# Half tiles of V as the unit of flow in a graph layer kernel

## What is computed

```python
h = relu(layernorm(x, axis=-1))
q = einsum('c,bcn->bn', wq, h)
k = einsum('c,bcn->bn', wk, h)
scores = q[:, None, :] + k[:, :, None]
scores = where(scores > 0, scores, 0.01 * scores)
att = softmax(scores, axis=-1)
agg = einsum('bcn,bmn->bcm', h, att)
out = x + relu(einsum('oc,bcm->bom', adj, agg) + bm[None, :, None])
```

## Time and profile before

| | us |
|---|---|
| median of 3 runs | 2064.33 |
| lowest, highest | 2063.56, 2064.44 |
| the profiled execution | 2065.63 |
| its span (first to last instruction) | 2063.6 |

### The profile page before, as it was taken

How to read it: one execution, slowest core, us unless ns; L and a number is a source line. 1 busy time by engine, 2 the same in 40 slices (tenths; PEclk the granted TensorE clock), 3 DMA queues, 4 the chain that set the end, 5 groups by cost and what they waited for, 6 DMA issues and landing times.

```text
span 2063.6 us, 37759 instructions
## 1 busy us (share of the span) xinstructions
PE 2035.2 (99%) x12467; PEld 1210.0 (59%) x12467; DVE 1721.7 (83%) x3631; ACT 1244.1 (60%) x2120; POOL 368.1 (18%) x272
## 2 busy tenths in 40 slices
PE   6999999999999999999999999999999999999999
PEld 5556556665566665566655666655666556666554
DVE  8988888888898888898888988888888889888863
ACT  5655756656656556566566565565665666655634
POOL 1012211112211122111121111221111211112212
PEclk9999999999999999999999999999999999999999
DMA  5244433334324444233443244442334432334322
GB/s 191 77 141 144 161 107 117 133 138 163 141 81 146 139 146 159 100 124 133 138 163 134 86 143 137 154 156 98 128 134 138 163 128 92 143 130 160 117 92 77
DMA packets 125119, 271.00 MB, mean 131 GB/s; under 512 B 21592, under 2 KB 22112, under 8 KB 120928
## 3 DMA queue, kind: packets, MB, share of 16 engines
q1 hardware_dynamic: 124480, 270.06, 37.8%
q10 hardware_dynamic: 544, 0.01, 0.0%
HBM read 202.38 MB, written 67.63 MB: 131 GB/s over the span
## 4 chain that ended last, share of the span: by engine, by line
PE 95%; DVE 3%; ACT 1%; DMA 1%; issue 0%; POOL 0%; SPq 0%; DVEq 0%; POOLq 0%
PE pair L450 21%; PE pair L451 21%; PE pair L452 21%; PE pair L421 11%; PE pair L426 10%; PE pair L424 10%; DVE den_out L794 1%; DMA ab_row<-ab_rows 0%; PE pair L344 0%; DVE p_ring L815 0%; ACT p_ring L546 0%; DMA xs<-in_x_dram 0%; PE small L399 0%; DVE v_lo L827 0%; DVE p_lo L822 0%
## 5 line engine op out<-in xcount | busy, mean ns | idle before, releaser
L450 PE MATMUL pair<-p_hi,v_hi 128*128 128x512 f16 x2048 | 776.4, 379 | 2.6 <-DVE p_lo L822 1.9
L452 PE MATMUL pair<-p_hi,v_lo 128*128 128x512 f16 x2048 | 776.2, 379 | 0.0
L451 PE MATMUL pair<-p_lo,v_hi 128*128 128x512 f16 x2048 | 776.2, 379 | 0.0
L997 POOL TENSOR_TENSOR res<-res,y 128x512 f32<-128x512 f32 x255 | 361.1, 1416 | 1674.5 <-ACT y L572 1674.5
L815 DVE SCALAR_TENSOR_TENSOR p_ring<-ab_row,cols,p_ring 128x512 f32<-128x512 f32 x512 | 376.6, 747 | 127.2 <-ACT p_ring L546 127.2
L794 DVE SCALAR_TENSOR_TENSOR den_out<-den_row,cols 128x512 f32<-128x512 f32 x512 | 440.7, 925 | 0.0
L546 ACT ACTIVATE p_ring<-ab_row,cols 128x512 f32<-128x512 f32 x512 | 353.2, 699 | 125.7 <-DMA ab_row<-ab_rows 125.7
L421 PE MATMUL pair<-wmT_hi,h_hi 128*128 128x258 f16 x2016 | 388.4, 273 | 3.1 <-ACT y L572 2.9
L424 PE MATMUL pair<-wmT_lo,h_hi 128*128 128x258 f16 x2016 | 386.6, 273 | 0.0
L426 PE MATMUL pair<-wmT_hi,h_lo 128*128 128x258 f16 x2016 | 386.5, 273 | 0.0
L822 DVE SCALAR_TENSOR_TENSOR p_lo<-p_ring,p_hi 128x512 f16<-128x512 f32 x512 | 349.7, 686 | 36.5 <-ACT p_hi L554 33.0
(11 more groups left out here) (97 smaller groups left out, 937.6 us busy)
## 6 DMA issues: line engine op xcount, KB each, us to landing
res<-in_x_dram SPq DMA_DIRECT2D x256, 256.0 KB, 3.3
out_dram<-res SPq DMA_DIRECT2D x256, 256.0 KB, 2.6
xs<-in_x_dram SPq DMA_DIRECT2D x124, 512.0 KB, 6.6
den_row<-den_rows SPq DMA_DIRECT2D x32, 1024.0 KB, 4.7
ab_row<-ab_rows SPq DMA_DIRECT2D x64, 512.0 KB, 4.8
res<-in_x_dram SPq DMA_DIRECT2D x4, 512.0 KB, 9.3
wm_nat<-in_adj_dram SPq DMA_DIRECT2D x4, 256.0 KB, 7.8
den_rows<-cols SPq DMA_DIRECT2D x32, 8.0 KB, 1.6
```

The lines of the kernel that those rows point to most:

```text
L450: pe.matmul(ps[:, :], v_hi[:, b[1], nt, chans], p_hi[:, hf, nt, :], start=(nt == 0), stop=False)
L451: pe.matmul(ps[:, :], v_hi[:, b[1], nt, chans], p_lo[:, hf, nt, :], start=False, stop=False)
L452: mm = pe.matmul(ps[:, :], v_lo[:, b[1], nt, chans], p_hi[:, hf, nt, :], start=False, stop=(nt == NT - 1))
L997: pool.tensor_tensor(res[:, k, :], res[:, k, :], y[:, k % 2, :], ALU.add).then_inc(s_add, 1)
```

## The change

Each bank of a V tile becomes a unit of its own. PE finishes the 12 matmuls of half 0 before those of half 1, and each half's last matmul increments s_v. ScalarE copies each half by itself (v_upper), VectorE splits each half by itself (v_lower), with one semaphore for each of the four banks, and PE waits for the bank alone before it writes to it again. The units 0 to 3 wait for their own bank (s_vlo[k]); unit 0's first two node tiles now wait for both halves of their V tiles. The start-up tiles (first_pass, second_pass, second_tiles, not shown) are signalled by half in the same way; their matmuls keep their order. In the first period alone, ScalarE does relus 5 and 6 before the two first leaks and relu 7 behind them, where they stood among the P tiles.

```diff
--- before.py
+++ after.py
@@ -181,7 +181,7 @@
         s_plo = sem("p_lo_ready")
         s_v = sem("v_psum_done")
         s_vhi = sem("v_hi_ready")
-        s_vlo = [sem(f"v_split_{i}") for i in range(2)]
+        s_vlo = [sem(f"v_split_{i}") for i in range(4)]
         s_acc = sem("unit_accumulated")
         s_y = [sem(f"relu_done_{i}") for i in range(2)]
         s_add = sem("unit_finished")
...
@@ -409,23 +409,19 @@
 
                 if nt == 0:
                     pe.wait_ge(s_hlo, cnt(b, CT, CT))
-                if nt < 2:
-                    for i in range(2):
-                        wait(pe, s_y[i], cnt(b, U // 2, nt + 3 - U))
-                else:
-                    pe.wait_ge(s_vlo[nt % 2], cnt(b, NT // 2, nt // 2))
                 ps, nodes = pair[nt % 2], slice(nt * P, (nt + 1) * P)
-                for ct in range(CT):
-                    hi, lo = h_hi[:, b[1], ct, nodes], h_lo[:, b[1], ct, nodes]
-                    for half, cols_of in enumerate((OH + QK, OH)):
-                        pe.matmul(ps[:, half, 0:cols_of], hi, wmT_hi[:, ct, half, 0:cols_of],
-                                  start=(ct == 0), stop=False)
-                    for half, cols_of in enumerate((OH + QK, OH)):
-                        pe.matmul(ps[:, half, 0:cols_of], hi, wmT_lo[:, ct, half, 0:cols_of], start=False, stop=False)
-                    for half, cols_of in enumerate((OH + QK, OH)):
-                        mm = pe.matmul(ps[:, half, 0:cols_of], lo, wmT_hi[:, ct, half, 0:cols_of],
-                                       start=False, stop=(ct == CT - 1))
-                mm.then_inc(s_v, 1)
+                for half, cols_of in enumerate((OH + QK, OH)):
+                    if nt < 2:
+                        wait(pe, s_y[half], cnt(b, U // 2, nt + 3 - U))
+                    else:
+                        pe.wait_ge(s_vlo[2 * (nt % 2) + half], cnt(b, NT // 2, nt // 2))
+                    for ct in range(CT):
+                        hi, lo = h_hi[:, b[1], ct, nodes], h_lo[:, b[1], ct, nodes]
+                        bank, w_hi, w_lo = ps[:, half, 0:cols_of], wmT_hi[:, ct, half, 0:cols_of], wmT_lo[:, ct, half, 0:cols_of]
+                        pe.matmul(bank, hi, w_hi, start=(ct == 0), stop=False)
+                        pe.matmul(bank, hi, w_lo, start=False, stop=False)
+                        mm = pe.matmul(bank, lo, w_hi, start=False, stop=(ct == CT - 1))
+                    mm.then_inc(s_v, 1)
 
             def unit(b, k, one, two):
 
@@ -434,7 +430,7 @@
                 if k >= MIX:
                     pe.wait_ge(s_y[k % 2], cnt(b, U // 2, (k - MIX) // 2 + 1))
                 elif one:
-                    pe.wait_ge(s_vlo[k // 2], cnt(nxt(b), NT // 2, NT // 2))
+                    pe.wait_ge(s_vlo[k], cnt(nxt(b), NT // 2, NT // 2))
                 else:
                     pe.wait_ge(s_y[k % 2], cnt(b, U // 2, (k + MIX) // 2 + 1 - U // 2))
                 ps, chans = mix[k % MIX], slice(ot * P, (ot + 1) * P)
@@ -444,7 +440,8 @@
                     if one and (k, nt) == ((1, 2) if at(b, first) else (0, 3)):
                         spread_qmax(nxt(b))
                     if k == 0 and nt < 2:
-                        pe.wait_ge(s_vlo[nt], cnt(b, NT // 2, NT // 2))
+                        for half in range(2):
+                            pe.wait_ge(s_vlo[2 * nt + half], cnt(b, NT // 2, NT // 2))
                     if ot == 0:
                         pe.wait_ge(s_plo, cnt(b, G, NT * hf + nt + 1))
                     pe.matmul(ps[:, :], v_hi[:, b[1], nt, chans], p_hi[:, hf, nt, :], start=(nt == 0), stop=False)
@@ -515,7 +512,7 @@
 
                 if ct == 0:
                     act.wait_ge(s_ln, cnt(b, LN_OPS, LN_OPS))
-                    wait(act, s_v, cnt(b, NT, -NT))
+                    wait(act, s_v, cnt(b, 2 * NT, -2 * NT))
                 src = x_second if at(b, second) else xs
                 act.activation(h_hi[:, b[1], ct, :], src[:, ct, :], ACT.Relu, bias=ln_shift[:, b[1], ct:ct + 1],
                                scale=ln_scale[:, b[1], ct:ct + 1]).then_inc(s_hhi, 1)
@@ -555,12 +552,13 @@
 
             def v_upper(b, nt):
 
-                act.wait_ge(s_v, cnt(b, NT, nt + 1))
-                ps = pair[nt % 2]
-                if not at(b, first):
-                    act.activation(qk4[:, nt, :], ps[:, 0, OH:OH + QK], ACT.Copy)
-                act.activation(v_hi[:, b[1], nt, :].rearrange("p (h o) -> p h o", h=2), ps[:, :, 0:OH], ACT.Copy,
-                               scale=1.0 / H_SCALE).then_inc(s_vhi, 1)
+                for half in range(2):
+                    act.wait_ge(s_v, cnt(b, 2 * NT, 2 * nt + half + 1))
+                    bank = pair[nt % 2][:, half, :]
+                    if half == 0 and not at(b, first):
+                        act.activation(qk4[:, nt, :], bank[:, OH:OH + QK], ACT.Copy)
+                    act.activation(v_hi[:, b[1], nt, half * OH:(half + 1) * OH], bank[:, 0:OH], ACT.Copy,
+                                   scale=1.0 / H_SCALE).then_inc(s_vhi, 1)
 
             def relu(b, k):
                 hf, ot = divmod(k, OT)
@@ -602,17 +600,22 @@
                 relu(b, 4)
                 if one:
                     n = nxt(b)
+                    if at(b, first):
+                        relu(b, 5)
+                        relu(b, 6)
                     leak(n, 0)
                     leak(n, 1)
+                    if at(b, first):
+                        relu(b, 7)
                     for nt in range(NT):
                         p_upper(n, nt)
                         if nt < NT - 2:
                             leak(n, nt + 2)
-                        if nt == 0:
+                        if nt == 0 and not at(b, first):
                             relu(b, 5)
-                        if nt == (1 if two else 3):
+                        if nt == (1 if two else 3) and not at(b, first):
                             relu(b, 6)
-                        if nt == (3 if two else 5):
+                        if nt == (3 if two else 5) and not at(b, first):
                             relu(b, 7)
                         if two and nt in (4, 6):
                             v_upper(h, nt // 2 - 2)
@@ -768,7 +771,7 @@
                     dve.wait_ge(s_qf, 2)
                     dve.wait_ge(s_un, 1)
                 else:
-                    dve.wait_ge(s_vhi, cnt(b, NT, NT))
+                    dve.wait_ge(s_vhi, cnt(b, 2 * NT, 2 * NT))
                 q_link(b, 1, dve.tensor_scalar(qk[:, 0, :], qk4[:, :, 0], unscale_q[:, 0:1], None, ALU.mult))
                 dve.tensor_scalar(qk[:, 1, :], qk4[:, :, 1], unscale_q[:, 1:2], None, ALU.mult).then_inc(s_qc, 1)
                 dve.tensor_reduce(qmax_p[:, :], qk[:, 0, :], AX.X, ALU.max).then_inc(s_qc, 1)
@@ -823,11 +826,12 @@
                                          in1=p_hi[:, hf, nt, :], op0=ALU.mult, op1=ALU.subtract).then_inc(s_plo, 1)
 
             def v_lower(b, nt):
-                dve.wait_ge(s_vhi, cnt(b, NT, nt + 1))
-                dve.scalar_tensor_tensor(out=v_lo[:, b[1], nt, :].rearrange("p (h o) -> p h o", h=2),
-                                         in0=pair[nt % 2][:, :, 0:OH], scalar=1.0 / H_SCALE,
-                                         in1=v_hi[:, b[1], nt, :].rearrange("p (h o) -> p h o", h=2),
-                                         op0=ALU.mult, op1=ALU.subtract).then_inc(s_vlo[nt % 2], 1)
+                for half in range(2):
+                    chans = slice(half * OH, (half + 1) * OH)
+                    dve.wait_ge(s_vhi, cnt(b, 2 * NT, 2 * nt + half + 1))
+                    dve.scalar_tensor_tensor(out=v_lo[:, b[1], nt, chans], in0=pair[nt % 2][:, half, 0:OH],
+                                             scalar=1.0 / H_SCALE, in1=v_hi[:, b[1], nt, chans], op0=ALU.mult,
+                                             op1=ALU.subtract).then_inc(s_vlo[2 * (nt % 2) + half], 1)
 
             def half_0(b, two):
                 weight(b, 0)
```

More of the change, by code:

```diff
@@ L340, in first_qk, with first_pass @@
                 return mm
-            def first_pass(nt, ct, h, w, start=False, stop=False):
+            def first_pass(nt, ct, h, w, start=False, stop=False, done=False):
                 for half in range(2):
@@ L345, in first_pass @@
                                    start=start, stop=stop)
-                return mm
+                    if done:
+                        mm.then_inc(s_v, 1)
             def first_tiles():
@@ L367, in first_tiles @@
                 for ct in range(CT):
-                    mm = first_pass(0, ct, h_lo, wmT_hi, stop=(ct == CT - 1))
-                mm.then_inc(s_v, 1)
+                    first_pass(0, ct, h_lo, wmT_hi, stop=(ct == CT - 1), done=(ct == CT - 1))
                 for ct in range(CT):
@@ L373, in first_tiles, with second_pass @@
                 for ct in range(CT):
-                    mm = first_pass(1, ct, h_lo, wmT_hi, stop=(ct == CT - 1))
-                mm.then_inc(s_v, 1)
```

(33 more changed lines are left out.)

## The result

The changed kernel takes 2049.1 us (median of 4, 2048.38 to 2050.7) against 2063.94 for the kernel before beside it (median of 4): ratio 0.9927, 95% interval 0.9915 to 0.9939. The profiled execution took 2049.04 us, its span 2047.3.

A forecast was written before the change was run, and what follows sets the result against it. PE, busy 2035.2 of 2063.6 us, was taken as the bound, with time lost where it waits. Terms -6.0 (seams), -1.2 (first period) and +0.3 (start-up) gave -6.9, so 2057.4 us from the median; range 2053 to 2063.5.

The forecast's parts named there:

- step 5: PE's order within a V tile, 12 matmuls in a row to one bank: no change; bounds -6.5 and +22 us.
- the faster rival: The fixed part of V matmuls falls to that of the units, -6.5 us: 2051 us, chance 0.08.
- Steps 1 and 2: Halves on ScalarE and VectorE: a half's copy lasts 0.38 us, a half's split 0.43 us.
- Steps 3 and 4: Late starts of unit 0 and of its transpose L399 go: 6.0 of 6.2 us saved.
- Both seams: V phase to unit 0, and transpose L399 in unit 0: PE loses 0.20 us a period on average.
- The lead of the split: Time in hand at unit 0, whose added waits were to lie within it: 0.6 us.
- seam A: V phase to unit 0, waiting for V tile 6's split behind the normaliser: 0.21 or 0.04 us late by turns.
- Step 6: Waits and signals by half in V tiles: gives nothing in steady periods.
- the rival of the increment: Eight more increments a period hold up the next matmul, taking 0.2 us a period: 2063.9 us, chance 0.04.
- Step 7: Moved relus of the first period: earlier V phase start, then waits of 2.4 and perhaps 0.5 us; 1.2 us saved.
- Step 8: Start-up: some four added VectorE instructions stand before the last h_lo, +0.3 us.

The follow-up runs named there:

- order alone: Kernel before with only PE's order in main-path V tiles changed, 12 matmuls of half 0 then 12 of half 1: 2057.99 us, ratio 0.9972.
- the padded kernel: Kernel before with the weights' rows padded from 258 to 288 columns, each moving slice starting at a multiple of 64 bytes: 2057.06 us, ratio 0.9967.
- the one with equal offsets: Kernel before with rows of 288 columns used from the third on, every slice 4 bytes past a multiple of 64: 2058.18 us, ratio 0.9966.
- halves without the order: Changed kernel with PE's old order inside a V tile, signals, copies, splits and waits by half kept: 2055.67 us, ratio 0.9957.
- that experiment: Changed kernel with relus 5, 6 and 7 of the first period back among the P tiles: 2048.58 us, ratio 0.9923.

## Why the prediction was wrong, step by step

**The step that failed is step 5.** It saw the right numbers: fixed part 3.7 ns in V matmuls, 2.6 in units, and a bound of -6.5 us if the first fell to the second. It took "no change", and the faster rival got 0.08. Measured is that bound: 21.28 to 21.06 a V phase, 0.22 x 31 = 6.8 us. The argument was that the slices are the same and that units pay nothing for staying on one bank, so that nothing was left that could change. The kernel with PE's order alone shows that the order sets the pace (21.07); the padded kernel and the one with equal offsets show what the step missed: the cost lies in the pair of neighbours, in their offsets, not in the slice and not in the bank. The 1.1 ns excess was a question that the trace put, and one look at the two tensors' strides (516 bytes against 1024 for the units' slices) would have given it a cause to weigh. With the forecast's other terms and this one, 2057.4 - 6.8 = 2050.6, against 2049.1.

The rival of the faster pace was priced at 2051, and the range began at 2053: it left out the very number that it gave this rival. The sum with the right term stays 1.5 above the measured time, and the start-ups of the two profiled executions alone differ by as much.

**Steps 1 and 2, right.** A copy of a half lasts 0.39 (forecast 0.38), a split of a half 0.417 (0.43), as the two groups of the changed kernel say:

```profile
L560 ACT ACTIVATE v_hi<-pair 128x256 f16<-128x256 f32 x512 | 189.8, 390 | 166.0 <-PE pair L423 161.2
L832 DVE SCALAR_TENSOR_TENSOR v_lo<-pair,v_hi 128x256 f16<-128x256 f32 x512 | 199.7, 417 | 76.6 <-ACT v_hi L560 76.0
```

**Steps 3 and 4, right.** Both seams are shut in every steady period; 0.22 a period, where 0.20 was forecast (the period fell by 0.44, of which 0.22 is pace). The lead of the split is 0.95 where 0.6 was reckoned. The added waits of unit 0 cost nothing that shows. What the prediction didn't say is that the seams needed less than they got: with PE's new order, ScalarE's halves alone do for both in the steady periods, VectorE's halves alone only for seam A.

**Step 6 and the rival of the increment.** At one order of PE, 16 increments a V phase in place of 8 make no difference: 21.06 against 21.07 in the new order (changed kernel and order alone), 21.28 against 21.28 in the old one (halves without the order, and before). So an increment in this steady stream is free, also in the middle of a tile. The number that the Trainium skill has for it ("TensorE: Matmul & The Clock Gate", The cost: per-tile semaphore tail) is some 26 ns for each increment in the tail behind a group of packed matmuls. Eight more at that price would be 0.21 a phase, an estimate from that page, and these runs have no room for it.

**Step 7, right in its mechanism.** PE starts the first V phase at its units' end and stops at tiles 2 and 3, for 2.17 and 0.37 us, where 2.4 and perhaps 0.5 were forecast; the clock didn't fall (1.00 in the window 116.34 to 140.30). The rows answer:

```profile
116.34 0.27 PE L421 MATMUL pair<-wmT_hi,h_hi 128*128 128x258 f16 x1
...
123.94 0.28 PE L421 MATMUL pair<-wmT_hi,h_hi 128*128 128x258 f16 x1 [2.17 <-DVE v_lo L832]
...
127.12 0.28 PE L421 MATMUL pair<-wmT_hi,h_hi 128*128 128x258 f16 x1 [0.37 <-DVE v_lo L832]
```

The stretch from first unit to second batch's first unit fell by 1.9, where 1.2 was forecast. Of it 0.2 is pace, and 1.2 goes back with the relus in the trace of that experiment, though not in its median; the rest isn't taken apart.

**Step 8** can't be judged: +0.3 is less than the start-up's scatter of 3 us between profiles.

## What to carry to other kernels

When PE is 99% busy, the pace of the matmuls is a term of its own: reckon start to start per matmul, subtract the columns at the granted clock, and compare the rest between stages; a stage with 1 ns more per matmul has a cause, and a reordering may remove or add it. Give the slices of a moving operand that follow each other a stride that is a multiple of 16 bytes: the padded rows gave 6.7 us here (float16 slices of 256 and 258 columns, 95% interval 4.3 to 9.5), with the arithmetic and the order as they were. And where a chain's last link decides a seam, halve the link that stands first behind PE; but before moving a step into another phase, reckon the slack of every step queued behind it.

## What the runs showed of the hardware

The cost of neighbouring moving slices at different offsets within 16 bytes was not expected: 0.24 us on 192 matmuls, 1.25 ns each, if every slice starts 4 or 12 bytes off its predecessor's offset (21.28 against 21.04). In the new order, where 16 changes of a V phase are of that kind and 48 are of 8 bytes, it is 0.02 us (21.06). Whether steps of 8 bytes are free, and why the change of offset costs time, stays open. With one offset, or with steps of 16 bytes, a matmul of 258 and one of 256 columns together take 0.219 us (21.04 / 96), which is 514 columns at 2.4 GHz and 2.5 ns for each of the two.
